# A ViT tower with relative attention and an eight-expert layer: the relative-value products, the output products and the first expert block in another order

## The reference, cut to what matters

```
attn = softmax((q k^T + q rel_k[idx]) / sqrt(c))
w1 = einsum('bhqk,bhkd->bhqd', attn, rv)
w2 = einsum('bhqk,qkd->bhqd', attn, rel_v[idx])       # the relative values
h = h + (w1 + w2) @ Wo + bo                           # the output product and the residual
xf = layernorm(h)
probs = softmax(xf @ Wr.T + br); the two largest of each row weigh the experts (comb)
y = sum over e of comb[:, e] * (gelu(xf @ W1[e] + b1[e]) @ W2[e] + b2[e])
h = h + y
```

## Time and profile before

| | us |
|---|---|
| median of 3 runs | 251.25 |
| lowest, highest | 250.98, 252.55 |
| profiled execution: span from first to last instruction | 249.9 |

### The profile page before, as it was taken

How to read it: one execution, slowest core, us unless ns; L and a number is a source line. 1 busy time by engine, 2 the same in 40 slices (tenths; PEclk the granted TensorE clock), 3 DMA queues, 4 the chain that set the end, 5 groups by cost and what they waited for, 6 DMA issues and landing times.

```text
span 249.9 us, 6298 instructions
## 1 busy us (share of the span) xinstructions
PE 230.9 (92%) x2316; PEld 194.7 (78%) x2316; DVE 191.3 (77%) x481; ACT 164.2 (66%) x509; POOL 62.8 (25%) x94
## 2 busy tenths in 40 slices
PE   1999999999998889989989999999899999999993
PEld 1945665899776766658778899889799999999972
DVE  1576789865668899998186738678999989989991
ACT  2461469752199899993026987422799888898870
POOL 8814132096005465469112400000000000000000
PEclk9999999999999999999999999999999999999999
DMA  6980000000003326064000000069888510001011
GB/s 147 335 217 3 1 0 1 3 3 0 3 0 81 91 65 108 4 212 129 3 7 3 0 3 0 8 103 131 151 211 260 173 37 10 22 4 32 0 42 34
DMA packets 15625, 16.46 MB, mean 66 GB/s; under 512 B 1747, under 2 KB 14367, under 8 KB 15468
## 3 DMA queue, kind: packets, MB, share of 16 engines
q1 hardware_dynamic: 14424, 15.59, 26.0%
q0 software_dynamic: 544, 0.35, 0.6%
q10 hardware_dynamic: 628, 0.14, 0.3%
HBM read 13.91 MB, written 2.16 MB: 64 GB/s over the span
## 4 chain that ended last, share of the span: by engine, by line
PE 54%; DVE 13%; issue 11%; POOL 11%; DMA 4%; ACT 3%; SPq 2%; DVEq 0%; POOLq 0%
PE banks L1328 49%; POOL region_e L471 5%; DMA region_d<-in_L_tok_W_sw 4%; DVE KT L1286 2%; POOL w_lo L526 2%; DVE top L1028 1%; DVE stb L992 1%; POOL region_d L478 1%; PE banks L1531 1%; POOL rstd L413 1%; PE banks L1672 1%; DVE stb L911 1%; ACT region_d L701 1%; DVE y_lo L1269 1%; DVE stats L890 1%
## 5 line engine op out<-in xcount | busy, mean ns | idle before, releaser
L760 ACT ACTIVATE w_sb<-banks,vecs 128x416 f32<-128x416 f32 x60 | 36.4, 608 | 11.2 <-PE banks L1328 8.9
L677 ACT ACTIVATE region_e<-banks,ntop 128x64 f32<-128x64 f32 x128 | 38.3, 346 | 5.0 <-DVE ntop L1035 4.8
L768 ACT ACTIVATE y_hi<-w_sb 128x416 fp32r<-128x416 f32 x60 | 32.7, 548 | 8.1 <-DVE w_sb L1260 8.1
L1269 DVE TENSOR_TENSOR y_lo<-w_sb,y_hi 128x416 fp32r<-128x416 f32 x60 | 34.9, 585 | 1.0 <-ACT y_hi L768 1.0
L677 ACT ACTIVATION_READ_ACCUMULATOR region_e<-banks,ntop 128x1 f32 x128 | 29.8, 238 | 0.0
L1328 PE MATMUL banks<-x_hi,w_hi 128*128 128x416 f32 x80 | 29.3, 366 | 0.0
L1328 PE MATMUL banks<-x_lo,w_hi 128*128 128x416 f32 x80 | 28.1, 352 | 0.0
L1328 PE MATMUL banks<-x_hi,w_lo 128*128 128x416 f32 x80 | 28.0, 350 | 0.0
L1260 DVE TENSOR_TENSOR w_sb<-w_sb,region_c 128x416 f32<-128x416 f32 x40 | 23.4, 586 | 2.5 <-ACT w_sb L760 1.0
L1328 PE MATMUL banks<-y_hi,w_hi 128*128 128x416 f32 x60 | 22.3, 371 | 1.5 <-DVE KT L1286 1.0
L1328 PE MATMUL banks<-y_hi,w_lo 128*128 128x416 f32 x60 | 21.1, 351 | 0.0
(11 more groups left out here) (238 smaller groups left out, 502.1 us busy)
## 6 DMA issues: line engine op xcount, KB each, us to landing
region_c<-out SPq DMA_DIRECT2D x4, 832.0 KB, 14.3
xnT<-out SPq DMA_DIRECT2D x5, 208.0 KB, 13.7
QT<-out SPq DMA_DIRECT2D x5, 208.0 KB, 14.1
region_a<-in_x SPq DMA_DIRECT2D x2, 512.0 KB, 5.3
region_a<-in_x SPq DMA_DIRECT2D x1, 1024.0 KB, 9.5
out<-h SPq DMA_DIRECT2D x2, 512.0 KB, 5.8
h<-out SPq DMA_DIRECT2D x4, 256.0 KB, 5.0
w_sb<-in_L_ffn_W SPq DMA_DIRECT2D x1, 1024.0 KB, 5.6
```

The costliest lines, as they stand in the source:

```text
L677: last = a.activation(dst[:, h // 2, h % 2], src[:, h // 2, h % 2], ACT.Exp, scale=SCALE, bias=ntop[:, o + h:o + h + 1], accum_out=esum[:, ...
L760: a.activation(lifted(u), bank[h_bank(i)][:, 0:FB], ACT.Gelu, bias=vecs[:, b:b + 1])\
L768: a.activation(h_hi(u), lifted(u), ACT.Copy).then_inc(S["hi_ok"], 1)
L1269: v.tensor_tensor(h_lo(u), lifted(u), h_hi(u).bitcast(F32), ALU.subtract).then_inc(S["lo_ok"], 1)
```

## The change

Five things, all in code that is written in order:

1. `REL_BANKS` and `OP_BANKS`: `relative(3)` writes bank 4 instead of bank 0 and waits for `attended(0)`, which reads that bank; `project(3)` writes bank 6 instead of 5; the class rows move from the banks 4 and 6 to bank 5. Bank 0 is thereby not used by these products, and `up(0, 0)`, which writes the banks 0 and 1, no longer waits for `o_ok` 4 (`attended(3)`); that wait moves to `router(0)`.
2. DVE: `residual(0)` ahead of `attended(1)`, `low(0)` ahead of `attended(3)`, `residual(3)` ahead of `low(1)`.
3. PE: no `filled`, and no `keep_warm(2)` ahead of `project(3)`.
4. PE: `relative(2)` whole ahead of `project(1)`; `turn2(0)` ahead of `project(2)`.
5. PE: `up(0, 0)` ahead of `project(3)`; `up(1, 0)` ahead of `turn2(1)` and `router(0)`.

```diff
@@ -57,8 +57,8 @@
 IN_BANKS = (6, 7, 0, 1)
 Y_BANKS = (3, 5, 4, 5)
 RING = 5
-OP_BANKS = (1, 2, 3, 5)
-REL_BANKS = (4, 5, 6, 0)
+OP_BANKS = (1, 2, 3, 6)
+REL_BANKS = (4, 5, 6, 4)
 CLS = 128 + M_ALL
 
 
@@ -1143,8 +1143,8 @@
             def attended_class():
 
                 dve.wait_ge(S["w2_ps"], 5)
-                link(v.tensor_tensor(OTc, bank[4][:, 0:IMG], OTc, ALU.add))
-                v.scalar_tensor_tensor(OTc, bank[4][:, IMG:2 * IMG], clsv[:, 5:6], OTc, op0=ALU.mult,
+                link(v.tensor_tensor(OTc, bank[5][:, 0:IMG], OTc, ALU.add))
+                v.scalar_tensor_tensor(OTc, bank[5][:, IMG:2 * IMG], clsv[:, 5:6], OTc, op0=ALU.mult,
                                        op1=ALU.add).then_inc(S["oc_ok"], 1)
 
             def residual(n):
@@ -1173,18 +1173,18 @@
                 normalise(KT, n, w, m, "rstd2_ok", "xn2D_ok", "x2T_ps", n - 1)
 
             attended(0)
+            residual(0)
             attended(1)
-            residual(0)
             attended(2)
             residual(1)
+            low(0)
             attended(3)
-            low(0)
             attended_class()
             residual(2)
+            residual(3)
             low(1)
-            residual(3)
             dve.wait_ge(S["opc_ps"], 1)
-            v.tensor_tensor(KT[0:IMG, TOK:TOK + C], bank[6][0:IMG, 0:C], clsr[0:IMG, :], ALU.add)\
+            v.tensor_tensor(KT[0:IMG, TOK:TOK + C], bank[5][0:IMG, C:2 * C], clsr[0:IMG, :], ALU.add)\
                 .then_inc(S["h1c_ok"], 1)
             residual(4)
             low(2)
@@ -1635,7 +1635,7 @@
                 if n == 2:
                     pe.wait_ge(S["w1_ev"], 8)
                 if n == 3:
-                    pe.wait_ge(S["pcx_ok"], 8)
+                    pe.wait_ge(S["o_ok"], 1)
                 for i in part:
                     q = 16 * n + i
                     for j in range(PJ):
@@ -1647,9 +1647,10 @@
             def relative_class():
 
                 pe.wait_ge(S["p0x_ok"], 1)
-                mm(bank[4][:, IMG:2 * IMG], kc[:, K_E8T:K_E8T + P], p0x[:, :])
+                pe.wait_ge(S["o_ok"], 2)
+                mm(bank[5][:, IMG:2 * IMG], kc[:, K_E8T:K_E8T + P], p0x[:, :])
                 for j in range(PJ):
-                    last = mm(bank[4][32 * j:32 * j + 32, 0:IMG], RVBD[:, 32 * NPATCH:32 * NPATCH + 32],
+                    last = mm(bank[5][32 * j:32 * j + 32, 0:IMG], RVBD[:, 32 * NPATCH:32 * NPATCH + 32],
                               PT[:, j, :, NPATCH])
                 last.then_inc(S["w2_ps"], 1)
 
@@ -1694,10 +1695,6 @@
                 last.then_inc(S["lg_ps"], 1)
 
             early, late = range(0, 8), range(8, 16)
-            def filled(n, part):
-                for i in range(part[0], part[-1] + 1, 4):
-                    relative(n, range(i, i + 4))
-                    keep_warm(1, spare=3)
 
             relative(0, range(0, 4))
             for p in range(PAIRS - 4, PAIRS - 2):
@@ -1706,31 +1703,29 @@
             turn_pc(7)
             for p in range(PAIRS - 2, PAIRS):
                 values(p)
-            filled(0, late)
-            filled(1, early)
+            relative(0, late)
+            relative(1, early)
             project(0)
             relative(1, late)
-            relative(2, early)
+            relative(2, range(16))
             project(1)
-            relative(2, late)
             relative(3, early)
+            turn2(0)
             project(2)
-            turn2(0)
             relative(3, late)
             relative_class()
+            pe.wait_ge(S["w1_split"], 1)
             pe.wait_ge(S["h1_ok"], 1)
-            keep_warm(2, spare=1)
+            pe.wait_ge(S["xlo_ok"], 1)
+            up(0, 0)
             project(3)
             pe.wait_ge(S["oc_ok"], 1)
-            mm(bank[6][0:IMG, 0:C], OTc, wo).then_inc(S["opc_ps"], 1)
-            pe.wait_ge(S["w1_split"], 1)
-            pe.wait_ge(S["o_ok"], 4)
-            pe.wait_ge(S["xlo_ok"], 1)
-            up(0, 0)
-            turn2(1)
-            router(0)
+            mm(bank[5][0:IMG, C:2 * C], OTc, wo).then_inc(S["opc_ps"], 1)
             pe.wait_ge(S["h1_ok"], 3)
             up(1, 0)
+            turn2(1)
+            pe.wait_ge(S["o_ok"], 4)
+            router(0)
             pe.wait_ge(S["xlo_ok"], 2)
             up(0, 1)
             turn2(2)
```

## The result

| | before | after |
|---|---|---|
| median, us | 251.12 (4 runs) | 254.16 (4 runs) |
| lowest, highest | 250.66, 252.55 | 254.01, 254.46 |
| span of the profiled execution | 249.9 | 252.5 |
| mean granted clock in it | 1.000 | 0.986 |

The ratio is 1.012, with a 95% interval of 1.0086 to 1.0154: 3.0 us more, where 252.4 with a range up to 253.5 was forecast. The other three executions of after have mean clocks of 0.992, 0.993 and 0.985. Ratios leave out executions more than 1.5% above the fastest of the same kernel, and for the changed kernel that can leave out just those in which the clock fell, so its medians over all executions and its clocks are given beside the ratio.

The account below looks back on a forecast made before the run. PE was taken as bound by its instruction supply in the dense stretch, so saved filler time became stops and up(0, 1) came 1.2 us later: span 249.9 + 1.2 = 251.1, with 1.35 to the median 252.4 (252.0 to 252.8; overall range 249.5 to 253.5).

Parts of the forecast that it names:

- The supply of instructions: PE's dense small products: 16 KB instruction packets arrive too slowly, so saved filler time becomes stops; chance 0.58, 252.4 us.
- Three 'issue' stops, ending near 120.25, 124.2 and 128.2: PE's weight loads: expected halts at packet crossings, the second 0.9 us and the third about 2 us long.
- the least distance between two crossings: PE's instruction packets: one crossing cannot follow the last by less than 3.95 to 4.0 us.
- The fillers: Removed PE products: 1.9 us among relative values plus 0.44 ahead of project(3), but only 0.4 us by packet supply.
- VectorE's order: DVE's reordering: turn2(0) ready at 128.1 but reached at 130.84, so 2.7 of the 3 us won not collected.
- the 0.51 of the text: PE's 0.51 us wait at 131.15 in before, forecast as all that the DVE reordering removes.
- about 1.4 us: PE's forecast idle time ahead of up(0, 1), where only router(0) is left as cover.
- PE's clock falls: Rival: without fillers and with more stops, PE's clock drops to half; 253.6 to 255.5 us, chance 0.13.
- in the third stop: Where the clock rival put the fall: the stop ending at 128.2, the clock low until 130.84, +2.6 us.
- a stop of 0.5 us beside 128 dense loads: Argument against the clock rival: in before, from 123.92, such loads without a filler kept the clock at 1.00.
- a crossing under 3.9 us: Stated test against the forecast: a packet crossing less than 3.9 us after the last would show it wrong.
- the 1.35 us from span to median: The profiled execution of before had a span 1.35 us below the median; the forecast kept that difference.

Follow-up runs that it names:

- e5: After unchanged, run again beside before: 255.05 us against 252.04, ratio 1.0075.
- e15: After with turn2(1) and router(0) ahead of up(1, 0), low(1) ahead of residual(3), the same kernel as e7 run again: 251.21 us, ratio 0.9967 to before.
- e3: Before without its four fillers among the relative values, in its own order: 252.06 us, ratio 0.9992 to before.
- e12: e7 with attended(1) again ahead of residual(0) on VectorE, as in before: 252.0 us, ratio 1.0002 to before.
- e16: After with one more wait (ve2_ok 5) ahead of up(0, 1), for a longer pause: 255.62 us, ratio 1.0129 to before.
- e14: After unchanged, run again in the fourth set: 254.88 us against 251.83 of before, twelve executions.
- e7: After with turn2(1) and router(0) ahead of up(1, 0), and low(1) ahead of residual(3): 251.11 us against 252.04 of before, ratio 0.9954.
- e9: After unchanged, run again in the third set: 250.97 and 256.03 us against 251.94 of before.
- e10: After unchanged, run again in the third set: 252.0 and 259.66 us against 251.94 of before.

## Why the prediction was wrong, step by step

*The supply of instructions: right in kind, its size taken as fixed.* "Three 'issue' stops, ending near 120.25, 124.2 and 128.2" came at 120.04, 123.66 and 127.11, at the loads named. The term that was mis-sized is the least distance between two crossings, "3.95 to 4.0 us": it was 3.62 and 3.45 here. In other executions the same lists gave 3.34 and 3.73 (e5) and 3.89 and 4.00 (e15), so it is not a constant of the chip that one profile could give. The third stop ended 1.1 us earlier than forecast (1.48 us long for 2.0), and everything behind it came 1.1 to 1.2 us earlier: `project(1)` 127.47 for 128.6, `turn2(0)` 129.65 for 130.84, `up(0, 0)` 132.81 for 134.0, `turn2(1)` 136.43 for 137.6, `up(0, 1)` 139.18 for 140.4. From the third stop to `up(0, 1)` the sum said 12.2 us, and it took 12.07: the list itself was added up rightly. By this term alone the forecast would have been 1.2 us too high, no change against before.

*The fillers: right for the new order, priced too low in the old one.* They were said to be paid for in stops, all but 0.4 us. In after, where the stops are 3.20 us for 1.18 before, none of the 1.9 is left at `up(0, 1)`. e3 took the four out of before and gained 1.09 in the one profile, with crossings 3.62 and 3.72 apart: the least distance again, not a fixed 3.95.

*VectorE's order: right that most of its gain is not collected.* `residual(0)` at 122.52 (122.7 forecast), `norm2(0)` 126.22 (126.4), `turn2(0)` without a wait for ScalarE. e12's wait of 0.62 us, in one profile, is near the 0.51 of the text.

*The clock: the step that failed.* The sum took the idle time ahead of `up(0, 1)` ("about 1.4 us"; 1.27 measured) at its face price and let the clock stand at 1.00 behind it. The rival "PE's clock falls" had the right mechanism and the right side, with a chance of 0.13, but put it "in the third stop", and argued against it from a stop of 0.5 us beside 128 dense loads. The row that bore on it was not a stop of before; it was the forecast's own new pause, behind three stops and one small gap (0.20), longer than any idle time of PE that the rows of before show in this stretch. The price was taken for 2.64 us of work at half speed; the low clock held for 6.8 us. Placed behind the pause, at the 2.6 to 3.0 us that the long falls of after and e16 show and with no gain from the order, the same rival reads 251.25 + 2.6 to 3.0, 253.9 to 254.3. "Wrong would be ... a granted clock under 1.00" was the test that came true, and so did "a crossing under 3.9 us".

*Two errors of opposite sign met.* The supply gave 1.2 us back, the clock took 2.6 to 3.0; the 1.35 us from span to median, kept in the sum, was 1.66 in after. The executions of after with a mean clock over 0.993 took 250.27, 250.97, 251.35 and 252.00 (and 429.41): as long as before, which is what the order alone is worth.

**A version without the pause.** e7, the change with `turn2(1)` and `router(0)` ahead of `up(1, 0)` and `low(1)` ahead of `residual(3)`, has medians of 251.11 and 251.21, 0.9 and 0.6 us under before and some 3.8 under after. Against before it is a gain of about 0.4% (0.9954, 0.9915 to 0.9993; the second time 0.9967, 0.9928 to 1.0005, which does not exclude none).

## What to carry to other kernels

An idle time of PE is not worth its length alone: ask what the clock does behind it, and a pause that the change creates has two prices, the waiting and, in the executions where the clock falls behind it, the work done at the lower level (here 1.4 to 3.0 us). When two products that hide a chain of copies are put in another order, check that something long still stands between the turn and the product that needs its result, on PE and on the engine that makes the last copy. And a period read off one profile, like that of the instruction packets, needs the spread of several before a sum rests on it.

## What was not expected of the hardware

- The same program with the same gaps has it both ways. After's first profile and e14 have identical stops (1.15, 0.57, 1.48) and pauses (1.27), and the clock is low for 6.8 us in one and 3.4 in the other; e9 differs only in the middle stop (0.29) and has none, and e10, with longer stops (1.15, 0.85, 1.75) and the same pause, has none either. The Trainium skill, TensorE: Matmul & The Clock Gate, Part 1, says that the gate's monitor runs freely and does not restart with a kernel, so that one kernel differs from run to run; the runs agree that it differs, and none of them sets the phase.
- Behind `up(0, 1)` the fall came when PE was at work again, not in the pause: 0.9 us after its start in after (140.1 for 139.18) and in e16 (141.0 for 140.11), 0.1 in e14 (141.5 for 141.42). It lasted while PE was busy throughout. That is no rule: the early fall of e5 began at 19.1, inside a wait that ended at 19.55.
- The stops of one program differ by 1.4 us between executions: 0.88, 0.30 and 1.76 in e7, 1.43, 0.84 and 2.04 in e15, and `up(0, 1)` comes 1.38 us later for it (23.77 for 22.39). The Trainium skill, Runtime: NRT & Kernel Launch, section "Instruction fetch mechanics", calls the crossing of a block mostly hidden; in this dense stretch each profile of after and of its variants shows crossings as stops of 0.3 to 2.0 us.
